# Selective scan of a decoder layer: delta rows spread by TensorE instead of DMA, five of sixteen C products on GpSimd, last layer's weights loaded in two parts, instruction orders rewritten

## The reference

```python
x = _layernorm(x + gated_linear_recurrence_block(x))          # layer 0
x = _layernorm(x + cross_attention(x, ctx))
x = _layernorm(x + latent_attention_and_mixture_of_experts(x))  # 16 heads, 7 routed + 1 shared expert
x = _layernorm(x + selective_scan(x))                          # layer 1
x = _layernorm(x + film_and_s4d_and_mlp(x, ctx))               # convolution by FFT, then 128-512-128
x = _layernorm(x + mixture_of_experts(x))                      # 8 routed of width 176, and a shared one
```

```python
delta = softplus(x @ Wd.T + bd)                 # (l, 128)
Bmat, Cmat = x @ Wb.T + bb, x @ Wc.T + bc       # (l, 16)
A_bar = exp(delta[..., None] * A)               # (l, 128, 16)
Bx = (delta * x)[..., None] * Bmat[:, :, None, :]
h[t] = A_bar[t] * h[t-1] + Bx[t]                # for each of 128 channels x 16 states
y[t] = sum_n h[t, :, n] * Cmat[t, n]
```

## Time and profile before

| | |
|---|---|
| median of 3 runs | 495.65 us (495.21 to 497.56) |
| span of the profiled execution | 494.8 us; the profile gives no time of its own beside it, so the 0.85 us up to the median stand for what lies around the span |
| mean granted TensorE clock | 0.934 of full speed |
| busy: TensorE, VectorE, ScalarE, GpSimd | 417.6, 335.1, 302.1, 123.7 us |
| DMA | 42.39 MB |

### The profile page before, as it was taken

The page is one execution under the profiler, slowest core; times in us unless marked ns, Lnnn a source line. Parts: engine busy times, 40 slices in busy tenths (PEclk is TensorE's granted clock), DMA queues, the critical chain, the costliest instruction groups (busy, mean ns, idle before and its releaser), DMA issues.

```text
span 494.8 us, 5930 instructions
## 1 busy us (share of the span) xinstructions
PE 417.6 (84%) x2049; PEld 203.1 (41%) x2049; DVE 335.1 (68%) x616; ACT 302.1 (61%) x513; POOL 123.7 (25%) x129
## 2 busy tenths in 40 slices
PE   6979868778979999978876874677699899999995
PEld 3535422353335554424332321425466644444442
DVE  2497776488877842745888997998965453554453
ACT  5648795514246679896788885554336687822443
POOL 1100460000420054058729484555020000000000
PEclk9999999959999999989996997668979999999999
DMA  7950000733280000023028778989300000000000
GB/s 266 338 168 15 1 2 0 200 54 148 70 186 5 3 3 1 3 63 108 0 69 208 190 177 229 212 228 273 157 0 1 1 0 1 0 1 0 1 21 21
DMA packets 23613, 42.39 MB, mean 86 GB/s; under 512 B 6965, under 2 KB 12310, under 8 KB 22422
## 3 DMA queue, kind: packets, MB, share of 16 engines
q1 hardware_dynamic: 23476, 41.92, 30.3%
q10 hardware_dynamic: 108, 0.10, 0.1%
HBM read 36.93 MB, written 4.98 MB: 85 GB/s over the span
## 4 chain that ended last, share of the span: by engine, by line
PE 55%; DVE 20%; ACT 8%; POOL 6%; issue 5%; DMA 5%; SPq 0%; DVEq 0%; ACTq 0%; POOLq 0%
DVE AR L1520 7%; PE PS L900 6%; PE PS L927 6%; PE PS L905 6%; ACT AR L1178 5%; PE PS L814 4%; PE PS L828 4%; DVE AR L1841 3%; POOL AR L2158 3%; PE PS L797 3%; PE PS L664 3%; DVE AR L1526 2%; DMA AR<-scan 2%; PE PS L1031 2%; DVE stats L1529 1%
## 5 line engine op out<-in xcount | busy, mean ns | idle before, releaser
L1178 ACT ACTIVATE AR<-PS 128x512 f32<-128x512 f32 (+2 forms) x185 | 98.4, 562 | 99.4 <-PE PS L900 44.2
L1520 DVE TENSOR_TENSOR AR<-PS,AR 128x512 f32<-128x512 f32 (+1 forms) x120 | 79.8, 678 | 57.6 <-PE PS L905 27.7
L2158 POOL TENSOR_TENSOR AR<-AR 128x512 f32<-128x512 f32 (+2 forms) x48 | 53.7, 1129 | 90.9 <-DVE AR L1520 60.0
L1178 ACT ACTIVATE AR<-AR 128x256 f32<-128x256 f32 (+3 forms) x110 | 46.9, 462 | 44.4 <-DVE AR L1520 28.6
L1174 ACT ACT_TABLE_LOAD x49 | 62.9, 1283 | 0.9
L1529 DVE TENSOR_REDUCE stats<-PS 128x1 f32<-128x128 f32 (+4 forms) x88 | 43.6, 525 | 11.5 <-PE PS L800 6.9
L1841 DVE TENSOR_TENSOR_SCAN AR<-PS,AR 128x512 f32<-128x512 f32 x32 | 38.9, 1214 | 2.2 <-ACT PS L1178 2.2
L797 PE MATMUL PS<-RR 97*128 97x512 bf16 (+3 forms) x128 | 31.9, 322 | 6.4 <-DVE stats L1529 3.3
L664 PE MATMUL PS<-AR,W_sq 128*128 128x256 f32 x88 | 26.6, 413 | 12.4 <-ACT AR L1178 7.9
L2244 POOL TENSOR_TENSOR RR<-KL,lags 128x512 f32<-128x512 f32 x24 | 26.6, 1146 | 40.0 <-PE PS L817 39.9
L814 PE MATMUL PS<-RR 100*128 100x512 bf16 (+3 forms) x128 | 29.9, 306 | 1.4 <-ACT AR L1178 1.1
...
## 6 DMA issues: line engine op xcount, KB each, us to landing
AR<-scan SPq DMA_DIRECT2D x64, 256.0 KB, 4.1
RR<-in_ffn SPq DMA_DIRECT2D x1, 2688.0 KB, 10.9
...
```

What stands on the lines that cost most here:

```text
L1178: nc.scalar.activation(out_, in_, func, bias=bias, scale=scale).then_inc(*done("act", *step))
L1520: nc.vector.tensor_tensor(out_, a, b_, op).then_inc(*done("dve", *step))
L2158: nc.gpsimd.tensor_tensor(out_, a, b_, op).then_inc(*done("pool", *step))
```

## The change

1. **Delta rows by TensorE.** The transfers of kind "dl" go: one of two writes and 16 of 32 spreads for each lane. In their place delta is split into three bf16 parts: `dh` (copy, ScalarE), `dr` (VectorE), `dm` (copy, ScalarE), `dn` (VectorE). For each tile three bf16 matmuls (`dp{i}`, K = 32, 512 columns) with a 0/1 matrix `chosen` write the sum of the parts, spread over 128 partitions, into the PSUM bank, and `aa{i}` works there in place. `dp{i}` waits for `sc{i-2}`. The matrix is made once in lane w (`se` on VectorE, `sd` on GpSimd).
2. **"dx" rows** stay with DMA, with five tiles on their way instead of four.
3. **C products.** `hc1`, `hc4`, `hc7`, `hc10`, `hc13` of each lane go to GpSimd, each placed behind `by` of two tiles later. They read a copy of C in SBUF (`bD`, ScalarE, once for each lane). The scan writes into a ring of seven tiles, and the product is made in place.
4. **Last layer's weights.** The gate part (896 KB) and `sel1` go where layer 0's attention weights were, as soon as those are free; the two other parts (1792 KB in two transfers) go to RA, issued between the last spread of lane a and the first write of lane b.
5. **Orders.** All strings of `TURNS` and all of `TABLES` are new. `TABLES` has 39 entries instead of 49.

The core of the diff (of the strings one line each):

```diff
+POOLED = (1, 4, 7, 10, 13)
+RING = (14, 15, 0, 1, 8, 7, 10)
-AHEAD = {"dl": 3, "dx": 4}
+AHEAD = 5
+DX_ROWS = (4, 5, 6, 11, 9)
...
-        "w39 b6 w13 a1 w2 a1 w1 a9 w1 a4 b1 a2 b16 w1",
+        "w20 b3 w1 b2 w3 b1 w27 a1 w3 a5 w1 a9 w1 a2 b1 a5 w1 b16 w1 b5",
...
+            sp.wait_ge(*after("pe", 1, "mo"))
+            sp.dma_start(ffn1_at["g"], dram["ffn1"][:, 0:E1N]).then_inc(loads["ffn1_g"], 16)
+            load("sel1", tiles["sel1"])
             def write_rows(b):
-                sp.wait_ge(*after("dve", b, "dl"))
-                sp.dma_start(rows_dram[b][0], A(b, 8)).then_inc(written["dl", b], 16)
                 sp.wait_ge(*after("pool", b, "dx"))
...
             write_rows(0)
             spread_rows(0, 0, NS)
+            sp.wait_ge(*after("pe", 1, f"fd{U0}"))
+            for k, name in ((1, "u"), (2, "d")):
+                sp.dma_start(ffn1_at[name], dram["ffn1"][:, k * E1N:k * E1N + E1N]).then_inc(loads["ffn1"], 16)
             write_rows(1)
...
             spread_rows(1, 7, NS)
-            load("ffn1", tiles["ffn1"])
-            load("sel1", tiles["sel1"])
...
+                for i in range(NS):                                  # TensorE
+                    if i >= 2:
+                        pe.wait_ge(*after("dve", b, f"sc{i - 2}"))
+                    for n, part in enumerate(delta_parts(b)):
+                        g = 32 * (i % 4)
+                        last = mm(own(b, 1 + 2 * (i % 2)), chosen[g:g + 32, 128 * (i // 4):128 * (i // 4) + 128],
+                                  part[g:g + 32, :], start=(n == 0), stop=(n == 2))
+                    last.then_inc(*done("pe", b, f"dp{i}"))
+                    yield
+                    if i >= 6 and not (i - 6) % SUMMED:
+                        sums((i - 6) // SUMMED)
+                        yield
...
                 for i in range(NS):                                  # ScalarE
-                    act.wait_ge(*spread_of(b, "dl", i))
+                    rows_ = own(b, 1 + 2 * (i % 2))
+                    act.wait_ge(*after("pe", b, f"dp{i}"))
...
+                hi, mid, lo = delta_parts(b)                         # VectorE
+                dve.wait_ge(*after("act", b, "dh"))
+                tt(A(b, 10), A(b, 8), hi, ALU.subtract, (b, "dr"))
+                dve.wait_ge(*after("act", b, "dm"))
+                tt(lo, A(b, 10), mid, ALU.subtract, (b, "dn"))
...
+                    k = i - 2                                        # GpSimd
+                    if k in POOLED:
+                        pool.wait_ge(*after("dve", b, f"sc{k}"))
+                        tt(weighted(b, k), weighted(b, k), A(b, 13), ALU.mult, (b, f"hc{k}"))
```

147 lines of the change are left out of this document (96 added, 51 removed), and 50 rows, old and new, of tables (TABLES, TURNS).

## The result

The changed kernel takes 516.08 us (median of four executions, 511.98 to 517.55) against 496.61 for the kernel before in the same comparison (495.21 to 498.68): a ratio of 1.0369, 95% interval 1.032 to 1.0417. It is 3.7% slower; 488.5 us was predicted. All later ratios are to the kernel before, measured on the same chip. For one experiment (`one_part`) three of eleven executions, at 504.6 to 505.5 us, are left out of the ratio as disturbed; with them its median is 499.37 against 497.47, a ratio of 1.0038.

The account below looks back on a forecast made before the run. VectorE was taken as the bound from 245 to 351.9 us, TensorE from 391 us on. Terms -3.0 + 3.0 - 4.0 - 3.0 = -7.0 us take 494.8 to 487.8, or 488.6 at the median; range 479 to 498.

Parts of the forecast that it names:

- Ahead of the scan: Stretch before 245 us: memset wait and table load gone, GpSimd's split longer; -3.0 us, bounds 0 and -5.
- From 245 us to b's first scan step: Stretch to 310.2 us: VectorE work +2.3 and more idle time from a later start; +3 us, bounds -2 and +9.
- The slip of a's `sc0`: Lane a's first scan step, behind b's routing and lane w's pieces on GpSimd, would come 3 to 9 us later.
- b's scan: Lane b's scan, to 351.9 us: five products leave VectorE, gaps halve, ed.c adds; -4.0 us, bounds -6 and +4.
- TensorE's own 96 new matmuls: In both scan stretches: 27 us (49 at half clock), fitting into TensorE's 30.8 us of free time.
- The gaps that were to halve: VectorE's gaps of 3.3 us in lane b's scan, mostly waits for exponentials, would halve: -1.7 us.
- TensorE's queue holds b's rows (slower): Rival: dp matmuls stand behind the other lane's waiting work in both scans; +12 us on the forecast, 500.5 us; chance 0.13.
- `ed.c` between b's tiles: In lane b's scan: 3.60 us on GpSimd between by12 and hc10, mostly covered by rows ahead; +0.8 us.
- The products on GpSimd: Five products by C of each lane leave VectorE in the scan stretches: -3.1 us a lane.
- Behind it: After b's scan: ed.s gone before b's next norm, -1.3, less TensorE idling, -1.7; -3.0 us, bounds 0 and -5.
- The earlier load is worth nothing by itself: Last layer's weights: they were there long before use already, so loading them earlier was put at no gain.
- the rival at 0.06: The weights' load stands in front of b's rows: first scan step up to 3.5 us late, 492 us; chance 0.06.

Follow-up runs that it names:

- one_part: Changed kernel with the old order for what had ended by 142 us, and one of three bf16 parts in each dp (32 matmuls, not 96): 1.0005.
- front40: Changed kernel with the old order, on all four engines, only for what had ended by 40 us: 507.70 us, 1.0219.
- early_rows: `front_back_late` with lane a's steps into its scan moved forward in the engines' orders: 505.71 us, 1.0187.
- rows_new_late_vector: `rows_new_late` with all products by C on VectorE again, leaving the new order of middle and tail on the old work: 503.69 us, 1.013.
- rows_new_late: Changed kernel with the front's old order, delta rows by DMA, weights' loads behind lane b's rows and ed behind b's scan: 501.54 us, 1.0083.
- front_back_late: Changed kernel with the old order up to 142 us, two weight loads behind lane b's last rows, and ed behind b's scan: 506.82 us, 1.0171.
- rows_new: Changed kernel with the old order up to 142 us and delta rows spread by DMA again: 504.65 us, 1.0122.
- rows_old_late: `rows_old` with the last layer's up and down weights loaded behind lane b's last rows: 499.85 us, 1.0042.
- tail_new: Changed kernel's work with the old orders for what had ended by 352 us and the new order behind: 537.31 us, 1.0828.
- rows_old: Kernel before in its own orders, with five products by C a lane on GpSimd and the last layer's weights loaded as in the change: 503.62 us, 1.0132.
- two_late: `front_back_late` with two of three bf16 parts (64 matmuls in place of 96) and without dn: 506.21 us, 1.0165.
- loose_banks: Changed kernel, old order up to 142 us; exponentials written to SBUF, dp waiting for an exponential instead of a scan step: 524.30 us, 1.0519.

## Why the prediction was wrong

**"Ahead of the scan", taken at -3.0, failed.** It was +9.0 up to a's `X3`, 7.7 of it by the end of a's maxima. The sum looked at the memset wait, the table load and the split, where the new order wins, and not at the start of the order, where it puts lane w's `m0` and `v0` ahead of a's `in0`, products for which TensorE is late. `front40` shows it: 1.5% from the first 40 us alone, with the spread said above. What of that is not VectorE's order stays open; the lower clock in the same stretch is one candidate, but no run separates it.

**"From 245 us to b's first scan step", +3 with bounds -2 and +9, held, but in part by luck.** It was +4.7 from a's `X3`. The slip of a's `sc0` behind `X3`, forecast at 3 to 9 us, was 5.9, and yet pulling a's rows forward brings nothing (`early_rows`). A part of the 4.7 is the new order, which costs 2.0 to 3.2 us there on the old work (`rows_new_late_vector`, `rows_new_late`). But 3.6 us of the stretch go with 64 of the matmuls (`one_part`) and 2.2 with the late load and `ed` (`front_back_late`), and both had been put at nothing there. That VectorE's one-input steps are not slowed by the products on GpSimd was right: 1215 ns for a scan step.

**"b's scan", -4.0 with bounds -6 and +4, failed by 13 us.** The step in it that failed is "TensorE's own 96 new matmuls cost 32 x 0.84 = 27 us (49 at half clock) and lie in its 30.8 us of free time in the two stretches". They took 31.9 us, near the lower price; but free time of an engine that works in order isn't where the new work stands. The gaps that were to halve, from 3.3 us to some 1.6, grew to 12.3 us of idle time (53.10 - 40.80), 8.0 of it waits of scan steps for exponentials. `one_part` shows that the amount costs: without 64 of them b's scan is 9.4 us shorter, 1.9 of them by `xin`, and the stretch ahead of it 3.6. The clock, which more work was not to lower, was 0.70 instead of 0.76, but it is 0.73 in `rows_new`, without any of the new matmuls. The rival "TensorE's queue holds b's rows (slower)", which got 0.13, names the right engine and comes near in size: +12 on the forecast for both lanes' scans, against 15 measured in the two stretches (4.7 and 9.3 for 3 and -4). The prediction's own sign for it, VectorE idle over 10 us in b's scan and released by exponentials that wait for a `dp`, came by and large. The changed kernel's timeline has the case that the rival described. `dp13`, whose bank is free when the scan step from 359.73 ends, stands behind 3.78 us of transforms (L1031), and its scan step waits 1.95 us; `dp14` behind the next transforms makes the following one wait 1.50:

```profile
359.73 1.22 DVE L1913 TENSOR_TENSOR_SCAN AR<-PS,AR 128x512 f32<-128x512 f32 x1 [1.30 <-ACT PS L1232]
359.87 3.78 PE L1031 MATMUL PS<-KL,RR 128*128 128x128 f32 x16
363.59 1.17 PE L1009 MATMUL PS<-AR,M 32*128 32x512 bf16 x3
...
364.79 0.67 ACT L1232 ACTIVATE PS<-PS,RA 128x512 f32<-128x512 f32 x1 [0.50 <-PE PS L1009]
365.49 1.22 DVE L1913 TENSOR_TENSOR_SCAN AR<-PS,AR 128x512 f32<-128x512 f32 x1 [1.95 <-ACT PS L1232]
```

Three of lane a's four `fl` do stand in front of `dp9` and `dp10` as well, but these two were in time: `xin` held VectorE longer. That meeting is a second step that failed. `ed.c` between b's tiles was put at +0.8, as time of GpSimd's queue; what it cost was 2.9 us of VectorE's `xin`, on which the sum had nothing, although it had reckoned with such meetings for `dr` and `dn`.

**The products on GpSimd**, -3.1 a lane, were mis-sized: three pairs of runs give 0.4 to 0.5% each, some 2.2 us for both lanes together, and no pair is clear of its intervals. From a's `X3` to the end their traces differ by 3.8, 2.3 and -1.2 us, and `rows_old_late` against the kernel before shows no gain. The work left VectorE, but VectorE wasn't short of time in scans that wait for rows or exponentials.

**"Behind it", -3.0, was right in sign and near in size, -4.9, but the mechanism was only in part the one given.** 3.6 us of it come from `ed` standing ahead (`front_back_late`), 1.3 of which the prediction had. Seen from TensorE, the other term, idling 1.7 us less, came out at 1.0, and 3.8 us are the same matmuls done in less time at a higher clock, which no term had. The order of the tail is worth 1.0 us at most (`tail_new`).

**"The earlier load is worth nothing by itself" and the rival at 0.06:** the load in front of b's rows costs 0.9% in the old orders (`rows_old_late`) and 0.85% in the new ones with three parts, there together with `ed`. Its price of up to 3.5 us was half of what was measured in `rows_old`, 6.8 us at b's first scan step; in the new orders with `ed` in its shadow it is 2.2.

**What stays open.** The parts don't add up: by the traces, from a's `X3` on, the late load gains 4.4 us with three parts and loses 4.4 with one. Of the 8.8 between, `lni.z` and `xin` make up 3.7; the rest is open, and so is why one part less gains nothing (`two_late`) and two parts less do. No two of these runs differ in the clock alone, so the clock's share isn't settled. Whether the short loop of scan step, `dp` and exponential costs anything beside TensorE's work is open too, since `loose_banks` slowed the scan step itself and `one_part` shortened both.
